# Two units' transposes together, a TensorE warm-up on a zero tile, and another order of the first normalisation and weight parts

## The reference

```python
mod = (_silu(L0_c) @ L0_wmod).reshape(L0_c.shape[0], 6, 1, -1)
sa, ca, ga, sb, cb, gb = ...
h = _layernorm(x, axis=-1) * (1 + ca) + sa
x = x + ga * _L0_attn_ref(h, L0_attn_weight_qkv, L0_attn_weight_proj)
h = _layernorm(x, axis=-1) * (1 + cb) + sb
x = x + gb * _L0_ffn_ref(h, ...)
# attention, per batch and group
scores = jnp.einsum('bsgqd,btgd->bgqst', q, k) * scale   # causal mask
attn = jax.nn.softmax(scores, axis=-1)
out = jnp.einsum('bgqst,btgd->bsgqd', attn, v)
```

## Time and profile before

| | us |
|---|---|
| median of 3 runs | 930.82 |
| lowest, highest | 930.01, 933.1 |
| the profiled execution | 929.75 |
| its span, first to last instruction | 927.9 |

### The profile page before, as it was taken

The page is one execution under the profiler, slowest core; times in us unless marked ns, Lnnn a source line. Parts: engine busy times, 40 slices in busy tenths (PEclk is TensorE's granted clock), DMA queues, the critical chain, the costliest instruction groups (busy, mean ns, idle before and its releaser), DMA issues.

```text
span 927.9 us, 15010 instructions
## 1 busy us (share of the span) xinstructions
PE 911.6 (98%) x5480; PEld 806.3 (87%) x5480; DVE 629.5 (68%) x1297; ACT 515.5 (56%) x1121; POOL 490.0 (53%) x699
## 2 busy tenths in 40 slices
PE   6989999999999999999999999999999999999997
PEld 5888889888898888888888888888888998888886
DVE  6568667865787578647875787378757776764554
ACT  4366556655766576547664766466647667531111
POOL 1576628671867186808671867166727989410000
PEclk9999999999999999999999999999999999999999
DMA  8000100000001000000010000000001001000000
GB/s 283 24 1 2 40 1 24 1 29 1 23 2 40 1 23 1 29 1 23 2 41 1 24 1 29 1 1 24 1 1 69 1 9 67 1 23 0 23 23 23
DMA packets 10180, 21.21 MB, mean 23 GB/s; under 512 B 1280, under 2 KB 5760, under 8 KB 9984
## 3 DMA queue, kind: packets, MB, share of 16 engines
q1 hardware_dynamic: 9392, 20.11, 6.3%
q10 hardware_dynamic: 720, 0.21, 0.1%
HBM read 18.22 MB, written 2.10 MB: 22 GB/s over the span
## 4 chain that ended last, share of the span: by engine, by line
PE 88%; DVE 3%; ACT 2%; POOL 1%; issue 1%; DVEq 0%; POOLq 0%
PE ps L1284 13%; PE ps L1127 12%; PE ps L1129 12%; PE ps L1128 12%; PE ps L1305 6%; PE ps L1302 6%; PE ps L1303 6%; PE ps L1267 6%; PE ps L1273 6%; PE ps L1270 6%; ACT prob L778 1%; DVE ps L1040 1%; ACT pt_hi L802 1%; DVE stats L881 1%; PE ps L1263 1%
## 5 line engine op out<-in xcount | busy, mean ns | idle before, releaser
L623 POOL TENSOR_TENSOR rinv<-rsum,mone 128x1 f32<-128x1 f32 x256 | 141.4, 552 | 232.0 <-ACT prob L778 231.4
L1044 DVE TENSOR_TENSOR pt_lo<-ps,pt_hi 128x512 fp32r<-128x512 f32 x288 | 198.2, 689 | 66.6 <-ACT pt_hi L802 63.4
L802 ACT ACTIVATE pt_hi<-ps 128x512 fp32r<-128x512 f32 x288 | 171.3, 598 | 118.2 <-PE ps L1284 115.8
L778 ACT ACTIVATE prob<-ps,nmax 128x256 f32<-128x256 f32 (+28 forms) x256 | 180.8, 706 | 84.2 <-DVE nmax L1040 82.4
L628 POOL TENSOR_SCALAR prob<-prob,rinv 128x256 f32<-128x256 f32 (+28 forms) x256 | 191.3, 747 | 38.8 <-POOL rinv L623 38.5
L1040 DVE CUSTOM_DVE_ANT_0 ps<-ps,mask_f 128x256 f32<-128x256 f32 (+28 forms) x256 | 183.1, 719 | 37.7 <-PE ps L1273 33.9
L1284 PE MATMUL ps<-ident,prob 128*128 128x128 f32 x1152 | 173.0, 274 | 2.7 <-POOL prob L628 2.4
L1284 PEld LDWEIGHTS ps<-ident,prob 128*128 128x128 f32 x1152 | 140.9, 141 | 22.8 <-DVE pt_lo L1044 4.0
L1302 PE MATMUL ps<-pt_hi,v_hi 128*128 128x512 f32 x288 | 134.3, 466 | 0.0
L1305 PE MATMUL ps<-pt_lo,v_hi 128*128 128x512 f32 x288 | 114.1, 396 | 0.0
L1303 PE MATMUL ps<-pt_hi,v_lo 128*128 128x512 f32 x288 | 113.4, 394 | 0.0
(11 more groups left out here) (179 smaller groups left out, 1815.8 us busy)
## 6 DMA issues: line engine op xcount, KB each, us to landing
w_raw<-in_wqkv SPq DMA_DIRECT2D x8, 640.0 KB, 3.9
wp_raw<-in_wproj SPq DMA_DIRECT2D x8, 512.0 KB, 3.5
out_y<-prob SPq DMA_DIRECT2D x8, 256.0 KB, 2.3
x<-in_x SPq DMA_DIRECT2D x3, 512.0 KB, 12.9
prob<-in_wug SPq DMA_DIRECT2D x3, 512.0 KB, 4.0
prob<-in_wmod SPq DMA_DIRECT2D x1, 1024.0 KB, 10.2
wv_raw<-in_wv SPq DMA_DIRECT2D x4, 256.0 KB, 4.3
raw_down<-in_wdn SPq DMA_DIRECT2D x1, 1024.0 KB, 4.8
```

What stands on the lines that cost most here:

```text
L778: a_.activation(row(i, h).rearrange("p (a n) -> p a n", a=nb), score_banks(i, h).rearrange("p (a n) -> p a n", a=nb)[:, :, 0:w], ACT.Exp, ...
L802: a_.activation(pt_hi[:, n % 3, :], ring(t, "T", n), ACT.Copy).then_inc(pth_done, 1)
L1044: v_.tensor_tensor(pt_lo[:, n % 3, :], ring(t, "T", n), pt_hi[:, n % 3, :].bitcast(F32), ALU.subtract).then_inc(ptl_done, 1)
```

## The change

It has four parts.

1. In `walk()`, the units go in pairs: T 2g, T 2g+1, then what stands "between", then V 2g, V 2g+1, then what stands "behind". What is "ahead" comes before the two T steps. Scores, chunks and the other steps get their places from `put()`: an even place is ahead of its pair, an odd one between. In the last turn, after row 5, the units go one by one again with a lag of two. ACT makes waiting exponentials after the second eviction of a pair only.
2. The four S steps of row 0 stand together behind Y of row 3 of the turn before, and VS and the other Y behind them. WP moves in the first turn from ahead of the scores of row 7 to between units 3 and V 2; in the later turns it comes before the scores of row 6.
3. `keep_running` gives PE matmuls on a 128x128 tile of zeros whose results nobody reads: 11 before the modulation, 3 and 5 behind the two first transposes, 4 before the first T of the first turn.
4. At the start ACT splits the first weights in two pieces (keys, then queries) and modulates slot 0 before them; DVE takes the variance of slot 1 after normalising slot 0.

```diff
@@ walk()
-CHUNKS_AT = [(4, 4, 3, 3), (3, 3, 2, 2)]
+CHUNKS_AT = [(3, 3, 3, 3, 2), (2, 2, 2, 2, 2)]
+def alone(t, n):
+    return t == TURNS - 1 and n > LAST[WINDOWS[2][0]] + 1
...
+        if t:
+            out += [(t - 1, "Y", WINDOWS[-1][1], 0)] + s0 + [(t, "VS", 0, 0), (t - 1, "Y", WINDOWS[-1][0], 0), (t, "WP", 0, 0)]
...
+        put([0, 1, 3, 5] if t else [1, 2, 3, 4], s6)
+        put([6, 7, 8, 9] if t else [5, 6, 7, 8], scores(t, 1))
+        put([9, 10, 11, 13], scores(t, 5))
+        put([14, 15, 16, 17], scores(t, 2))
+        put([18, 19, 21, 22], scores(t, 4))
+        put([23, 24, 25, 25], scores(t, 3))
+        put([9, 12, 15, 17], [(t, what, 0, 0) for what in ("LF", "LN", "LH", "LL")])
+        behind[7].append((t, "L", 0, 0))
+        if t == 0:
+            put([3], [(t, "WP", 0, 0)])
...
+            out += ahead[g] + [(t, "T", 2 * g, 0), (t, "T", 2 * g + 1, 0)] + between[g]
...
+            out += [(t, "V", 2 * g, 0), (t, "V", 2 * g + 1, 0)] + behind[g]
@@ scalar
+            act.wait_ge(mod_ok, 1)
+            ln_modulate(0, 0, 0, 0)
             act.wait_ge(wraw_s, 16)
-            a_.activation(w_hi[:, :, :], w_raw[:, :, :], ACT.Copy).then_inc(w_first_s, 1)
...
-                    if n != NU - 1:
+                    if n % 2 or alone(t, n):
                         exps()
@@ vector
-            for slot in range(2):
-                ln_normalise(0, 0, 0, slot)
+            ln_statistics(0, 0, 0, 1)
+            ln_normalise(0, 0, 0, 0)
+            ln_variance(0, 0, 0, 1)
@@ tensor
+            def keep_running(bank, count):
+                for _ in range(count):
+                    mm(bank[:, 0:P], nothing[:, :], nothing[:, :], start=True, stop=True)
+            pe.wait_ge(nothing_s, 1)
+            keep_running(S[1], 11)
...
-            for slot in range(2):
+            for slot, count in ((0, 3), (1, 5)):
                 ln_transpose(0, 0, 0, slot)
+                keep_running(S[1], count)
...
                     if t == n == 0:
+                        keep_running(T[1], 4)
```

More of the change, by code:

```diff
@@ L90, in walk @@
         out += [(0, "C", 5 + k, 0), (0, "GA", k, 0)]
-    out += [(0, "C", 9, 0), (0, "WM", 0, 0), (0, "WP", 0, 0), (0, "C", 10, 0)] + s7[:2]
+    out += [(0, "C", 9, 0), (0, "WM", 0, 0), (0, "C", 10, 0)] + s7[:2]
     out += [(0, "C", 11, 0)] + s7[2:] + [(0, "C", 12, 0), (0, "C", 13, 0)]
@@ L94, in walk @@
         s0, s6 = scores(t, 0), scores(t, NT - 2)
[L95 to L149, removed]
+        if t:
+            out += [(t - 1, "Y", WINDOWS[-1][1], 0)] + s0 + [(t, "VS", 0, 0), (t - 1, "Y", WINDOWS[-1][0], 0), (t, "WP", 0, 0)]
+        else:
+            out += s0 + [(t, "VS", 0, 0)]
+        ahead, between, behind = ([[] for _ in range(NU // 2)] for _ in range(3))
@@ new lines, in put @@
+        def put(places, items):
+            for n, item in zip(places, items):
+                (between if n % 2 else ahead)[n // 2].append(item)
+        put([0, 1, 3, 5] if t else [1, 2, 3, 4], s6)
[5 more added lines that the diff above has]
+        put([9, 12, 15, 17], [(t, what, 0, 0) for what in ("LF", "LN", "LH", "LL")])
@@ new lines, in walk @@
+        behind[7].append((t, "L", 0, 0))
+        if t == 0:
+            put([3], [(t, "WP", 0, 0)])
+        if t + 1 < TURNS:
+            put([21], [(t, "W", 0, 0)])
+            left = [(t + 1, "C", c, 0) for c in range(len(chunks(t + 1)))]
+            for k, many in enumerate(CHUNKS_AT[(t + 1) % 2]):
+                put([27 + k] * many, left)
+                del left[:many]
+            put([28], [(t + 1, "WM", 0, 0)])
+            put([32, 33, 34, 35], scores(t + 1, NT - 1))
+            if t == 1:
+                put(range(30, 35), [(t, "GB", k, 0) for k in range(5)])
+        else:
+            put([6, 13, 22], [(t, "B", k, 0) for k in range(3)])
@@ new lines, in walk @@
+        due = []
+        for g in range(NU // 2):
+            if alone(t, 2 * g):
+                continue
+            if 2 * g + 1 < NU - 1 and not (t + 1 == TURNS and g == 12):
+                between[g] += [(t, "Y", row, 0) for row in due]
+                due = []
+            due += [UNITS[n][0] for n in (2 * g, 2 * g + 1) if n == LAST[UNITS[n][0]]]
+            out += ahead[g] + [(t, "T", 2 * g, 0), (t, "T", 2 * g + 1, 0)] + between[g]
+            if alone(t, 2 * g + 2):
+                break
+            out += [(t, "V", 2 * g, 0), (t, "V", 2 * g + 1, 0)] + behind[g]
@@ L150, in walk @@
+        if t + 1 == TURNS:
+            first = LAST[WINDOWS[2][0]] + 2
+            for n in range(first, NU):
+                out += [(t, "T", n, 0)] + ([(t, "H", 0, 0)] if n == 32 else []) + [(t, "V", n - 2, 0)]
+                if n - 2 == LAST[WINDOWS[2][0]]:
+                    due = [(t, "Y", WINDOWS[2][0], 0)]
+                elif n == first + 2:
+                    out += due
+            out += [(t, "V", NU - 2, 0), (t, "V", NU - 1, 0)]
     for n, i in enumerate(WINDOWS[-1][::-1]):
@@ L230, in build @@
         mone = sb("mone", [P, 1])
+        nothing = sb("nothing", [P, P])
         su_u = sb("su_u", [P, KH])
@@ L522, in _ @@
             pool.sem_inc(wp_ready, 1)
+            g_.memset(nothing[:, :], 0.0).then_inc(nothing_s, 1)
             g_.memset(mone[:, :], -1.0)
```

32 lines of the change are left out of this document (21 added, 11 removed).

## The result

| | us |
|---|---|
| kernel before, median of 5 runs taken with it | 930.82 |
| changed kernel, median of 5 runs (957.32 to 959.09) | 958.23 |
| ratio, 95% interval | 1.029, 1.028 to 1.031 |
| the profiled execution, its span | 958.23, 956.4 |

Slower, as forecast, but 8 us above the forecast of 950 and 0.2 us outside the range.

The account below looks back on a forecast made before the run. PE was taken as always busy, its loads waiting 10.9 us after 60 us. From 929.75, new waits +29.6, old waits -8.5, V matmuls -1.6 and start +1.5 gave 950.75; forecast 950, range 942 to 958.

Parts of the forecast that it names:

- S 5.0: Scores behind T 8, T 9: wait for S 1.2's exponential, made behind both evictions; 1.1 in 7 turns, 7.7 us.
- S 2.1: Scores that wait for S 5.3's exponential, made behind row 1's `o_hi`; 0.6 in 8 turns, 4.6 us.
- L: T 17 and V 16: T 17 waits for L's bank (0.4), V 16 for `pt_lo` queued behind `h_hi` (0.6); 8 turns, 8.1 us.
- V 6 and V 22: Third V matmul waits for `pt_lo` after short steps between: 0.42 and 0.21 in each of 8 turns, 5.0 us.
- turn border: S 0.1 waits for S 7.3's exponential behind row 4's `o_hi`, V 0 slightly; 0.6 at 7 borders, 4.2 us.
- old waits gone: PE's weight-load waits for exponentials and `pt_lo` after 60 us, 10.9 us idle; 8.5 us taken as saved.
- V matmuls: Six V matmuls instead of three follow each group of transposes; 1.6 us saved, between 0 and 4.3.
- start and first turn: First chunks gain 0.6, but Y 0 waits for WP on POOL and the clock falls; +1.5, bounds -3.3 and +2.2.
- The lag argument: A third V matmul ends 1.91 us after its unit's transposes; pairs put too little between, so PE waits.
- b: Time of the step between a pair's T and V steps; PE waits where it is under 0.77 us.
- the clock's fall inside turns: Rival: PE's clock drops once a turn behind grouped transposes and a wait; 14 us more, 964; chance 0.05.
- waits share and halve: Rival: new waits are half as long because one late wait finds the next data ready; 936; chance 0.22.

Follow-up runs that it names:

- lh_late: Changed kernel with LH (DVE's high part of the second layer norm) moved from ahead of V 14 to behind S 2.3: 954.38 us.
- exp_first: Changed kernel with ACT making a waiting exponential ahead of `o_hi` of a finished row, not behind it: 975.35 us.
- port_gap: Changed kernel with one more wait on POOL, for DVE's first `g_lo` subtraction, ahead of its last butterfly: 956.53 us.
- last_old: Changed kernel with the last turn's units one by one in the old order of windows, B steps at their old places: 954.31 us.
- zero_only: Kernel before with the 23 zero-tile matmuls alone added: 928.23 us.
- wp_early: Changed kernel with the first turn's WP at its old place, ahead of chunk 10 and row 7's scores: 952.22 us.
- b_late: Changed kernel with POOL's third butterfly step of the last turn behind row 3's scores instead of ahead of them: 959.62 us.
- exps_each: Changed kernel with ACT making a waiting exponential behind each T step's eviction, not only behind a pair's second: 988.53 us.
- start_exp_first: Kernel before plus zero tile and new order of first normalisation and weight parts, with exponentials ahead of `o_hi`: 929.90 us.
- fixed_all: Changed kernel with row 1's scores earlier, LH behind S 2.3, exponentials behind each T, first turn's WP at old place, last turn in old order: 970.63 us.

## Why the prediction was off

Prices from the trace of the changed kernel beside the prediction's terms:

| term | predicted | measured |
|---|---|---|
| S 5.0, 7 times | 7.7 | 7.75 |
| S 2.1, 8 times | 4.6 | 4.6 |
| L: T 17 and V 16 | 8.1 | 3.7 + 3.8 = 7.6 |
| V 6 and V 22 | 5.0 | 3.5 + 1.7 = 5.1 |
| turn border | 4.2 | 3.0 |
| old waits gone | -8.5 | -9.2 |
| V matmuls | -1.6 | -1.9 |
| start and first turn | +1.5 | +3.0 (by difference) |
| C 1, T 27, V 35 | none | 1.9 + 0.8 + 1.1 |
| end of the last turn, MLP's start | none | 4.7 |
| sum | 21.0 | 28.5 |

The lag argument held: from b and the durations of a few rows, the named waits were put at 29.6 us and measured 28.1, and `lh_late` shows that the cause named for V 16, what is queued on DVE behind `h_hi`, is the right one. `exp_first` does the same for S 2.1, whose wait went. What failed is the step "New waits: 5.0 + 7.7 + 4.6 + 8.1 + 4.2 = 29.6 us", taken as complete. The sum is 7.5 us short: 4.7 at the end of the last turn and behind it, 3.8 at C 1, T 27 and V 35, and 1.5 at the start, less 2.5 in the terms that were taken too high or, for what goes, too low:

- **The last turn** was charged like the others, and what follows it was taken as unchanged. Unit by unit from T 28 on, it needs row 3's scores sooner, and POOL, which from 760 to 785 us idles 3.5 us for late exponentials, is 3.4 us further behind PE than before at the last scaling (V 25 ends at 788.20, the scaling at 794.50; before 765.17 and 768.03). 2.5 of the 4.7 us come from the DVE subtraction of 4.64 us, which took 0.68 before; `port_gap` shows that it hangs on POOL. The kernel before shows it only short, and whether it comes depends on how POOL and PE happen to stand to each other (below): this third of the miss is bad luck, the rest is not. `last_old` gives back 3.9.
- **C 1 and T 27.** A chunk's bank waits for S 3.3's exponential, T 27 in odd turns for S 4.3 behind W on POOL. The same chain (an exponential behind two evictions) was worked out for S 5.0 and S 2.1 but not for each score in a `between` place; C 1 is where the last one of the turn is read. V 35's 1.1 came in the turn with the GB steps on DVE; no run moves these steps, so that cause is not shown.
- **The start**: the first chunk came 0.9 later, not 0.5 earlier. The zero tile gave 2.0 (`zero_only`), more than the 0.6 taken, and at another place: it kept the clock at T 0. Y 0 then cost 6.0 (`wp_early`), where 3.7 of waiting (59 to 62.7) and 1.0 for the clock were taken. POOL had `wp_lo` at 64.33, not at 62.7. (The 3.46 taken for the split is the sum of its two steps; from 38.47 to 42.01 it is 3.54.)

Of the rivals, the clock's fall inside turns did not come: after 67.8 us it is full to the last matmuls. That waits share and halve did not come either: S 5.0 repeats at 1.10 to 1.11 us in seven turns and S 2.1 at 0.57 to 0.58 in eight. The others repeat nearly as well; the exceptions are V 16 in the last turn (0.60 in place of 0.46), one turn border (0.47 in place of 0.40) and C 1, which goes between 0.22 and 0.30.

## What to carry to other kernels

List the new order's waits by going through every step in a late place, not only those of the kind found first, and treat the first turn, the last turn and what follows it as cases of their own: most of the miss was there. Where an engine's queue serves several customers, a moved instruction is late for all of them (`b_late`, `exps_each`, `exp_first`, `start_exp_first`), so an edit is not safe to price by the one wait that it is meant to remove. Edits whose waits have separate causes did add: four of them gave 17.9 of 18.8 us (`fixed_all` against `exps_each`).
